# Patch embedding of a vision transformer: float32 products replaced by three float16 products, loads and one copy moved

## What is computed

```python
h = patches @ W_lin.T + b_lin; h = concat([cls, h])       # 197 tokens an image
x = layernorm(h)
q, k, v = split(x @ qkv_weight.T)                          # 12 heads of 16
attn = softmax(layer_norm(q) * SCALE @ layer_norm(k).T)
h = h + (attn @ v) @ proj_weight.T
h = h + experts(layernorm(h))                              # top 2 of 8, and a shared one
```

## Time and profile before

| | us |
|---|---|
| median of 3 runs | 1838.97 (1836.14 to 1839.57) |
| the profiled execution's own time | 1838.55 |
| its span | 1836.8 |

### The profile page before, as it was taken

The page is one execution under the profiler, slowest core; times in us unless marked ns, Lnnn a source line. Parts: engine busy times, 40 slices in busy tenths (PEclk is TensorE's granted clock), DMA queues, the critical chain, the costliest instruction groups (busy, mean ns, idle before and its releaser), DMA issues. The chain is left out here.

```text
span 1836.8 us, 43648 instructions
## 1 busy us (share of the span) xinstructions
PE 1756.6 (96%) x16914; PEld 1218.7 (66%) x16914; DVE 1213.8 (66%) x3497; ACT 977.9 (53%) x2078; POOL 302.9 (16%) x338
## 2 busy tenths in 40 slices
PE   3899999999999999999999959999999999999998
PEld 2677777777777777777777635555555555555555
DVE  4555555555555555555555438888888888888887
ACT  2555555555555555555555534545454545545453
POOL 0000000000000000000000003443434343444433
PEclk9999999999999999999999979999999999999999
DMA  5011111111111111111111010001010101000000
GB/s 186 2 51 51 51 51 51 52 51 42 45 51 51 51 51 51 52 51 45 44 48 51 11 37 27 27 27 35 19 36 18 36 18 36 21 33 27 24 18 15
DMA packets 31641, 75.67 MB, mean 41 GB/s; under 512 B 3467, under 2 KB 16430, under 8 KB 31310
## 3 DMA queue, kind: packets, MB, share of 16 engines
q1 hardware_dynamic: 31438, 72.89, 12.7%
HBM read 53.51 MB, written 19.37 MB: 40 GB/s over the span
## 5 line engine op out<-in xcount | busy, mean ns | idle before, releaser
L585 ACT ACTIVATE prob<-ps_sc 99x792 f32<-99x792 f32 x384 | 317.3, 827 | 88.2 <-PE ps_sc L427 88.2
L1216 POOL TENSOR_TENSOR in_lo<-inner,in_hi 128x512 f16<-128x512 f32 (+1 forms) x225 | 257.9, 1146 | 433.2 <-ACT act L1003 432.9
L372 PE MATMUL ps_hid<-lin_f,xin 128*99 128x192 f32 x1536 | 283.8, 328 | 32.2 <-DMA xin<-xp 28.1
L372 PEld LDWEIGHTS ps_hid<-lin_f,xin 128*99 128x99 f32 x1536 | 239.4, 167 | 33.4 <-DMA xin<-xp 28.1
L1149 DVE SCALAR_TENSOR_TENSOR acc<-ps_y,comb,acc 128x192 f32<-128x192 f32 (+1 forms) x700 | 242.0, 408 | 0.3 <-PE ps_y L945 0.3
L1011 ACT ACTIVATE in_hi<-inner 128x512 f16<-128x512 f32 (+1 forms) x225 | 140.3, 623 | 181.4 <-DVE inner L1131 181.4
L1003 ACT ACTIVATE act<-ps_h 128x512 f32<-128x512 f32 (+1 forms) x225 | 131.7, 585 | 189.3 <-PE ps_h L929 189.3
L943 PE MATMUL ps_y<-w_hi,in_hi 128*128 128x192 f16 (+1 forms) x900 | 223.9, 249 | 4.1 <-DVE acc L1149 2.6
L1131 DVE SCALAR_TENSOR_TENSOR inner<-ps_h,act 128x512 f32<-128x512 f32 (+1 forms) x225 | 153.8, 684 | 102.9 <-ACT act L1003 99.3
L945 PE MATMUL ps_y<-w_hi,in_lo 128*128 128x192 f16 (+1 forms) x900 | 221.4, 246 | 0.0
L944 PE MATMUL ps_y<-w_lo,in_hi 128*128 128x192 f16 (+1 forms) x900 | 221.4, 246 | 0.0
(11 more groups left out here) (148 smaller groups left out, 3198.0 us busy)
## 6 DMA issues: line engine op xcount, KB each, us to landing
xin<-xp SPq DMA_DIRECT2D x64, 594.0 KB, 4.3
hidden_dram<-h SPq DMA_DIRECT2D x64, 147.0 KB
hin<-hidden_dram SPq DMA_DIRECT2D x24, 384.0 KB, 3.0
out<-acc SPq DMA_DIRECT2D x24, 384.0 KB, 2.3
w_f<-w SPq DMA_DIRECT2D x1, 2304.0 KB, 9.9
hidden_dram<-h SPq DMA_DIRECT2D x64, 0.8 KB
w_f<-w SPq DMA_DIRECT2D x1, 864.0 KB, 11.5
qkv_f<-w_qkv SPq DMA_DIRECT2D x1, 576.0 KB, 3.9
```

The lines of the kernel that those rows point to most:

```text
L372: last = pe.matmul(hid[:, t, :], xin[q][:, k, t * TR:(t + 1) * TR], lin_f[:, k, :], start=(k == 0), stop=(k == PCHUNKS - 1))
L585: act.activation(prob[quad][:, places].rearrange("p h m s -> p h (m s)"), ps_sc[0:TR, places, 0:2 * SLOTS], ACT.Exp, scale=D ** -0.5 / (SQ ...
L1216: pool.tensor_tensor(in_lo[b][:, 0:N], inner[b][:, 0:N], in_hi[b][:, 0:N], ALU.subtract).then_inc(inlo_done, 1)
```

## The change

- The embedding weight is split in the prologue like the others (lin_hi, lin_lo); its load is the second of the queue.
- Each float32 product of the embedding becomes three float16 products, x_hi w_hi + x_hi w_lo + x_lo w_hi, 36 an image instead of 12.
- x_hi, the image's float16 high half, is loaded a second time from the same float32 input by a DMA from GpSimd that converts on the way, into three buffers; for image n it waits until image n-3 is embedded.
- x_lo = xin - x_hi is made by VectorE in two halves of 128x594, the first at the end of the step before, the second after xT_lo.
- hidden() divides by the weight's scale, in the same instruction that adds the bias.
- xin has three buffers instead of four; SP loads the first three ahead of the pipeline and then, in step k after the step's store, image k+3.
- VectorE's kT_copy(n3, 1) stands ahead of qk_variance(n2, 0).
- Phase A's buffers are released before phase B's are placed.

```diff
-        with ExitStack():
+        with ExitStack() as passing:
+            def sa(name, shape, dt=F32):
+                return passing.enter_context(nc.sbuf_tensor(name, shape, dt))
+
             def stage(name, shape):
-                return sb(name, shape)
+                return sa(name, shape)
 
             def split_pair(name, shape):
                 return sb(name + "_hi", shape, F16), sb(name + "_lo", shape, F16)
 
+            lin_hi, lin_lo = split_pair("lin", [128, PCHUNKS, C])
             qkv_hi, qkv_lo = split_pair("qkv", [128, 2, 3 * C])
             proj_hi, proj_lo = split_pair("proj", [128, 2, C])
...
-            weights = [(qkv_f, qkv_hi, qkv_lo, w_qkv),
+            weights = [(qkv_f, qkv_hi, qkv_lo, w_qkv), (lin_f, lin_hi, lin_lo, w_lin),
                        (proj_f, proj_hi, proj_lo, w_proj), (gate_f, gate_hi, gate_lo, w_gate),
                        (w13_f, w13_hi, w13_lo, w13), (w2_f, w2_hi, w2_lo, w2)]
             tailed = [qkv_f, proj_f, gate_f]
-            others = [(lin_f, w_lin), (id32, ident), (biascls, bias_cls), (gbias, gate_bias), (bef4, before4), (bef8, before8)]
...
+            others = [(id32, ident), (biascls, bias_cls), (gbias, gate_bias), (bef4, before4), (bef8, before8)]
+
+
+            xin = [sa(f"xin{p}", [128, PCHUNKS, SLOTS]) for p in range(3)]
+            x_hi = [sa(f"x_hi{p}", [128, PCHUNKS, SLOTS], F16) for p in range(3)]
+            x_lo = [sa(f"x_lo{p}", [128, PCHUNKS, SLOTS], F16) for p in range(2)]
+            h = [sa(f"h{p}", [TR, 2, C]) for p in range(HB)]
...
-        phase_a(nc, xp, hidden_dram, sem, locals())
+            phase_a(nc, xp, hidden_dram, sem, locals())
         phase_b(nc, hidden_dram, out, sem, sb, locals())
...
-        x_in = [sem(f"x_in{p}") for p in range(4)]
+        x_in = [sem(f"x_in{p}") for p in range(3)]
+        xhi_in = [sem(f"xhi_in{p}") for p in range(3)]
+        xlo_done = sem("xlo_done")
...
             def load(n):
-                q = n.mod(4)
-
-                if reached(n.times(1, -3)):
-                    sp.wait_ge(hid_done, n.times(1, -3))
+                q = n.mod(3)
+
+                if reached(n.times(2, -4)):
+                    sp.wait_ge(xlo_done, n.times(2, -4))
                 sp.dma_start(xin[q][:], xp[n.times(1)]).then_inc(x_in[q], 16)
...
             def step(k):
-                if k.active():
-                    load(k)
                 if k.back(5).active():
                     store(k.back(5))
-
+                if k.back(-3).active():
+                    load(k.back(-3))
+
+            for n in range(3):
+                load(Index(0, n))
             run(step)
...
-                q = n.mod(4)
+                hi, lo = x_hi[n.mod(3)], x_lo[n.mod(2)]
                 if part == 0:
-                    pe.wait_ge(x_in[q], n.quarters(16, 16))
+                    pe.wait_ge(xlo_done, n.times(2, 2))
...
                 for j in range(4 * part, 4 * part + 4):
                     t, k = j // PCHUNKS, j % PCHUNKS
-                    last = pe.matmul(hid[:, t, :], xin[q][:, k, t * TR:(t + 1) * TR], lin_f[:, k, :],
-                                     start=(k == 0), stop=(k == PCHUNKS - 1))
+                    s = slice(t * TR, (t + 1) * TR)
+                    pe.matmul(hid[:, t, :], hi[:, k, s], lin_hi[:, k, :], start=(k == 0), stop=False)
+                    pe.matmul(hid[:, t, :], hi[:, k, s], lin_lo[:, k, :], start=False, stop=False)
+                    last = pe.matmul(hid[:, t, :], lo[:, k, s], lin_hi[:, k, :], start=False,
+                                     stop=(k == PCHUNKS - 1))
                 if part == 2:
                     last.then_inc(hid_done, 1)
...
+            def split(n, half_no):
+
+                i = n.times(1)
+                if half_no == 0:
+                    dve.wait_ge(x_in[n.mod(3)], 16 * (i // 3 + 1))
+                    dve.wait_ge(xhi_in[n.mod(3)], 16 * (i // 3 + 1))
+                    if reached(n.times(1, -1)):
+                        dve.wait_ge(hid_done, n.times(1, -1))
+                ks = slice(3 * half_no, 3 * half_no + 3)
+                dve.tensor_tensor(x_lo[n.mod(2)][:, ks, :], xin[n.mod(3)][:, ks, :], x_hi[n.mod(3)][:, ks, :],
+                                  ALU.subtract).then_inc(xlo_done, 1)
+
             def hidden(n):
                 q = n.mod(HB)
                 dve.wait_ge(hid_done, n.times(1, 1))
 
                 if reached(n.times(1, 1 - HB)):
                     dve.wait_ge(h2_done, n.times(1, 1 - HB))
-                dve.tensor_tensor(h[q][:], hid, biascls[:], ALU.add).then_inc(h_done, 1)
+                dve.scalar_tensor_tensor(out=h[q][:], in0=hid, scalar=1.0 / SW, in1=biascls[:],
+                                         op0=ALU.mult, op1=ALU.add).then_inc(h_done, 1)
...
                     kT_copy(n3, 0)
                 if n2.active():
                     xT_out(n2)
-
+                if k.active():
+                    split(k, 1)
+
+                if n3.active():
+                    kT_copy(n3, 1)
                 if n2.active():
                     qk_variance(n2, 0)
-                if n3.active():
-                    kT_copy(n3, 1)
                 if n2.active():
                     qk_normalise(n2, 0)
                 if n1.active():
...
                 if n2.active():
                     v_copy(n2)
-
+                if k.back(-1).active():
+                    split(k.back(-1), 0)
+
+            split(Index(0, 0), 0)
             run(step)
+
+
+        @block.gpsimd
+        def _(pool):
+            def load_first(n):
+
+                if reached(n.times(1, -2)):
+                    pool.wait_ge(hid_done, n.times(1, -2))
+                pool.dma_start(x_hi[n.mod(3)][:], xp[n.times(1)]).then_inc(xhi_in[n.mod(3)], 16)
+
+            for k in range(IMAGES):
+                load_first(Index(0, k))
```

More of the change, by code:

```diff
@@ new lines, in vit_layer @@
+            xin = [sa(f"xin{p}", [128, PCHUNKS, SLOTS]) for p in range(3)]
+            x_hi = [sa(f"x_hi{p}", [128, PCHUNKS, SLOTS], F16) for p in range(3)]
+            x_lo = [sa(f"x_lo{p}", [128, PCHUNKS, SLOTS], F16) for p in range(2)]
+            h = [sa(f"h{p}", [TR, 2, C]) for p in range(HB)]
+            stats = sa("stats", [TR, 2, 6])
+            meanvar = sa("meanvar", [TR, 2, 2])
+            h_rstd = sa("h_rstd", [TR, 2])
+            h_lnvar = sa("h_lnvar", [TR, 2])
+            xnorm = sa("xnorm", [TR, 2, 256])
@@ new lines, in vit_layer @@
+            xT_hi = sa("xT_hi", [128, 2, SLOTS], F16)
+            xT_lo = sa("xT_lo", [128, 2, SLOTS], F16)
+            qk_sq = sa("qk_sq", [TR, 2 * HEADS, D])
+            qk_var = sa("qk_var", [TR, 2 * HEADS])
+            qk_lnvar = sa("qk_lnvar", [TR, 2 * HEADS])
+            qk_rstd = sa("qk_rstd", [TR, 2 * HEADS])
+            qk_norm = [sa(f"qk_norm{t}", [TR, 2 * HEADS, QB]) for t in range(2)]
+            qT = [sa(f"qT{p}", [128, QUADS, SLOTS]) for p in range(2)]
+            kT = [sa(f"kT{p}", [128, QUADS, SLOTS]) for p in range(2)]
@@ L175, in vit_layer @@
+            v = [sa(f"v{p}", [TR, 2, HEADS, VB]) for p in range(2)]
+            prob = [sa(f"prob{q}", [TR, QUAD, 2, SLOTS]) for q in range(QUADS)]
+            oT = [sa(f"oT{p}", [128, QUADS, SLOTS]) for p in range(2)]
+            o_rden = sa("o_rden", [TR, 2, HEADS])
+            o_norm = sa("o_norm", [TR, 2, 256])
+            onT_hi = sa("onT_hi", [128, 2, SLOTS], F16)
+            onT_lo = sa("onT_lo", [128, 2, SLOTS], F16)
+            h2 = [sa(f"h2{p}", [TR, 2, C]) for p in range(2)]
             w_loaded = [sem(f"w_loaded{n}") for n in range(len(weights))]
@@ L255, in _ @@
                     pool.wait_ge(consts_set, 1)
-        phase_a(nc, xp, hidden_dram, sem, locals())
+            phase_a(nc, xp, hidden_dram, sem, locals())
         phase_b(nc, hidden_dram, out, sem, sb, locals())
 def phase_a(nc, xp, hidden_dram, sem, bufs):
-    (lin_f, qkv_hi, qkv_lo, proj_hi, proj_lo, id32, biascls, eps, eps_qk, xin,
+    (lin_hi, lin_lo, x_hi, x_lo, qkv_hi, qkv_lo, proj_hi, proj_lo, id32, biascls, eps, eps_qk, xin,
      h, stats, meanvar, h_rstd, h_lnvar, xnorm, xT_hi, xT_lo, qk_sq, qk_var, qk_lnvar, qk_rstd,
@@ L270, in phase_a @@
         bufs[n] for n in (
-            "lin_f qkv_hi qkv_lo proj_hi proj_lo id32 biascls eps eps_qk xin "
+            "lin_hi lin_lo x_hi x_lo qkv_hi qkv_lo proj_hi proj_lo id32 biascls eps eps_qk xin "
             "h stats meanvar h_rstd h_lnvar xnorm xT_hi xT_lo qk_sq qk_var qk_lnvar qk_rstd "
```

## The result

| | before | after |
|---|---|---|
| median | 1837.68 us (4 runs, 1836.14 to 1839.57) | 1813.54 us (4 runs, 1810.96 to 1814.47) |
| profiled execution | 1838.55 | 1810.96 |
| its span | 1836.8 | 1809.2 |

The change makes the kernel 1.3% faster: ratio 0.9866, 95% interval 0.9849 to 0.9883. The medians are 24 us apart, the two profiled executions 27.6: the profiled one of after was the fastest of its four, with a mean granted clock of 0.991 where the other three have 0.988 to 0.989. The forecast was 1804, with 1786 to 1824 as its range.

The account below looks back on a forecast made before the run. TensorE was taken as the bound only with small margins, its saved time counting only where VectorE isn't next. 1838.55 - 39 (62 x 0.63) + 5 (prologue) = 1804.5, forecast 1804 us, range 1786 to 1824.

Parts of the forecast that it names:

- the residual's wait: Between project and attend: o_by_token would no longer wait for VectorE's residual, starting 0.20 us sooner.
- the filling: Phase A's first five steps, where TensorE waits for other engines: counted as three steps of 0.63 us gain.
- the first embedding: At phase A's start: its shorter time (6.75 us before) gives back at least 1 us, half beyond the 39.
- Part 1: TensorE's embedding: three float16 products per float32 product, 0.98 us a part against 1.31, saving 0.33 a part, 0.99 an image.
- Stretch one: TensorE from attend(n4, 1) to qk(n2, 0), 3.10 us: xT_lo holds qk back, so gain 0.06 of 0.33.
- Part 2: VectorE's kT copy ahead of the variance: scores(n3, 0) no longer waits for it; qk_var 0.12 us later, at most 0.20.
- The walk without the move: The same period estimate with kT still copied behind the variance: a period of about 15.5 us.
- Part 3: Two subtractions an image on VectorE, 0.78 us each (0.62 from below), both fitting in idle time and costing nothing.
- Part 4: Phase A's image loads: the converting load takes 4 to 10 us and, like the plain one, stays hidden.
- Rivals C and D: Slower: GpSimd holds VectorE up (1880 us, chance 0.06), or the converting load itself is slow (2098 us, chance 0.04).
- Part 5: Prologue: w_lin load 1.8 us, first loads 3 more, two subtractions 1.5; sum 6.3, net 5 after the give-back.
- Rival B: Phase A: VectorE chain later by 0.3 us a period, or float16 products at 0.10; period about 15.5, 1820 us, chance 0.20.

Follow-up runs that it names:

- the copy moved, alone: Kernel before the change, with only kT_copy(n3, 1) moved ahead of qk_variance(n2, 0): 1833.12 us, ratio 0.9972, period 15.83.
- the first image alone: Changed kernel, with both queues holding back the loads of images 1 and 2 until image 0's converting load has landed: 1814.43 us (one run).

## Why the prediction was right, and where its sizes were off

**The mechanism held.** That xT_lo and onT_lo hold TensorE back, so that only the first part's saving and the residual's wait count, was the core of it. The three stretches, forecast and measured:

| stretch | before | forecast gain | after | gain |
|---|---|---|---|---|
| attend to qk | 3.10 | 0.06 | 3.09 | 0.01 |
| qk to project | 5.54 | 0.0 | 5.52 | 0.02 |
| project to attend | 7.25 | 0.58 | 6.77 | 0.48 |
| period | 15.88 | 0.63 | 15.38 | 0.50 |

(The rows of "before" add up to 15.89, and the forecast gains to 0.64, through rounding.) The pauses came as foreseen too. Start to start, the step before qk is 0.31 longer than in the kernel before, the one before project 0.33, where a pause of some 0.3 and 0.4 was forecast. The experiments bear the mechanism out from both sides: products taken out beside xT_lo and onT_lo are worth nothing (15.39), products taken out of the first part count whole (15.05).

The whole account, in us less than before:

| stretch | forecast | measured |
|---|---|---|
| to the first product | -6.3 | -6.8 |
| to the first onT_lo | 3.2 | 1.4 |
| the next 59 steps | 37.2 | 28.7 |
| the last four steps | 0 | 4.5 |
| sum | 34 | 27.8 |

The forecast's 39 is 37.2 for the 59 full steps and 1.9 for the filling, to which it added 1.3 for the first embedding. So the steady part fell short by 8.5, 59 times the 0.14 by which the saving of a step was too large. The 4.5 of the last steps, for which the forecast had nothing, hid half of that. That the sum came so near is in this part luck.

**Part 1, the size of the saving.** 0.33 a part was too much. From embed(k, 0) to the next attend it took 1.39 before (602.57 to 603.96), and from embed(n1, 2) to scores 1.40 where scores waited for nothing else (the copy moved, alone). After, both take 1.09 (607.62 to 608.71, 612.88 to 613.97). So the saving is 0.30. I had read the float32 part up to a transpose (1.31) and the float16 part as 12 x 0.082, where ahead of scores or attend either takes some 0.1 more. The rest of the last stretch: the residual's wait gave 0.19 (2.79 to 2.60) for 0.20; the 0.06 that I booked before scores(n3, 2) didn't come, that stretch went from 1.80 to 1.82.

**Stretch one.** 0.05 for the signal from xT_lo to qk was a guess; it is 0.10 after and 0.11 before (606.95 to 607.06), so TensorE stood right at the end of it already. The row that gives it was in the earlier trace rows and I didn't read it off.

**Part 2** was right in direction: a chain that begins 0.13 later (qk_var starts 1.67 after qk instead of 1.54, for a forecast 0.12), for a wait of 0.36 less. The walk without the move gave about 15.5, the chip 15.58.

**Part 3** was right: 0.77 each for the forecast 0.78, both in idle time.

**Part 4** was right: 4.0 us in the range of 4 to 10, hidden. Rivals C and D are out. The rule of the Trainium skill beside rival C ("SBUF — State Buffer", section "SBUF: two separate sides") shows no effect here: xnorm's first instruction takes 0.38 as before, and the period is 15.38 with the converting loads and without. GpSimd's issue runs from 614.34 to 614.87, where VectorE waits and then starts qk_norm, which reads PSUM (614.64); xnorm comes at 617.58. How long the descriptors are being written stands in no trace, so no run here tests the rule.

**Part 5** came out at 6.8 for 6.3, by two errors that nearly cancel. The weight that now goes second in the queue moved ScalarE's release by 0.6 between the two traces (12.00 to 12.59), not by 1.8. Not even the 0.6 is safe: with the old order of loads the release stands at 12.00 and 12.77 (the copy moved alone), with the new one between 12.37 and 12.93 in the seven traces that have the changed kernel's prologue. The rate that I took from bytes over time was not what bound the large weight's landing; its time from issue to landing is 9.9 us in both profiles (9.8 to 10.7 in the others). What does bind it is open. The first loads took 4.65 more, for a forecast of 3 that rested on no row. Four other loads in flight are about 2 of that, as the experiment with the first image alone shows. The 1.3 that the forecast's sum gives back for the first embedding doesn't follow from its own words, "at least 1, half of it beyond what the 39 holds", which leave 0.5. From the first product to hidden it took 6.79 before and 5.99 after, 0.8 less. All of the filling gave 1.4, for the 3.2 in the table; the granted clock was 0.97 in it, 1.00 before.

**Draining** wasn't in the sum at all. The time from the 60th to the 64th onT_lo, with the granted clock of TensorE in that stretch:

| kernel | us | granted clock |
|---|---|---|
| before | 46.06 | 0.89 |
| the copy moved, alone | 45.69 | 0.85 |
| kT behind the variance again | 44.73 | 0.89 |
| changed | 41.53 | 0.97 |
| no converting loads after the third | 43.84 | 0.90 |

The last two run the same code there, since the embedding is over, and differ by 2.3 us. The clock differs with it. So of the 4.5 about half goes with a clock that stayed up in this trace, and some 2.2 are left for the shorter work. That a lower clock makes the steps longer is argued from these rows: no run sets the clock by itself. What else binds those steps is open.

**Rival B** (a period of 15.5, 1820) and the forecast (15.1 to 15.4, 1796 to 1813) stood at 0.20 and 0.59. The period fell at the upper end of the forecast's and the median just above its time, so between the two. The cause was a size, the saving of a part, and not one of those that B names: the float16 products do come at 0.082.

## What to carry to other kernels

Work taken off the busiest engine counts only where nothing else arrives at the same moment: for every start behind the shortened stretch, write down how late its other input is now, and give the saving only up to that. Read the length of a group as the distance to the same kind of instruction that follows it in that place, not to the one that is convenient. When the steady part is done, price the start and the drain by themselves: here the first loads, issued in the prologue instead of behind it, were worth 7 us, a quarter of what the whole change brought.

## What the runs showed of the hardware

- A float16 product of 128x99 weights and 192 columns takes 0.082 to 0.083 us start to start, and a float32 one 0.328. The Trainium skill ("FP8 and Floating Point Precision", section "TensorE Precision Notes") says that true float32 takes four passes through the array; the rows agree, with a ratio of 4.0.
- A load that converts 594 KB of float32 to 297 KB of float16, issued by GpSimd, lands in 4.0 us (median), no later than the plain load of the same source (4.4), and 61 of them cost nothing beside VectorE's and TensorE's work: 15.38 a period with and without.
- Three plain and three converting loads at once are another matter: the first pair is usable after 8.4 us, and after 6.3 with the other four held back.
- TensorE's granted clock, 1.00 (2.4 GHz) in the steady part, falls when phase A drains. In the kernel before it was 0.66 in the 10 us from 1034.7 on, between its two levels (1.2 and 2.4 GHz), after 10 us in which TensorE was busy for 8.9. In the changed kernel it stayed at 1.00 up to 1031.4.
